# Recurrent layers: v copied to the state partitions by DMA instead of matmuls, the product kept in PSUM, GpSimd's product tied to the next item

## The reference

```
xa = LN(x); sx = shifted xa - xa
xm_j = xa + sx * (maa_stack_j + tanh((xa + sx*maa_x) @ maa_w1)_j @ maa_w2_j)   # j: k, w, v, r, g
w = exp(-exp(time_decay + tanh(xw @ td_w1) @ td_w2)); r, k, v = xr@Wr.T, xk@Wk.T, xv@Wv.T
for t:                                   # a scan over the 100 tokens
    a   = k_t[:, None] * v_t[None, :]    # 16 x 16 per head
    out = r_t . (u * a + s)
    s   = a + w_t[:, None] * s
x1 = x + (head_norm(out) * silu(xg@Wg.T)) @ Wo.T
return x1 + sigmoid(xr2@Wfr.T) * (relu(xk2@Wfk.T)**2 @ Wfv.T)
```

## Time and profile before

| | us |
|---|---|
| median of 3 runs (3709.96 to 3715.34) | 3711.06 |
| the profiled execution | 3714.36 |
| its span in the trace | 3712.5 |
| first layer's recurrence, product of item 1 to product of item 128 | 861.12 to 1620.29 |
| a turn in the middle of a layer | 98.7 to 102.3 |

### The profile page before, as it was taken

How to read it: one execution, slowest core, us unless ns; L and a number is a source line. 1 busy time by engine, 2 the same in 40 slices (tenths; PEclk the granted TensorE clock), 3 DMA queues, 4 the chain that set the end, 5 groups by cost and what they waited for, 6 DMA issues and landing times.

```text
span 3712.5 us, 57293 instructions
## 1 busy us (share of the span) xinstructions
PE 3342.7 (90%) x19200; PEld 2542.2 (68%) x19200; DVE 2232.2 (60%) x5509; ACT 1484.0 (40%) x4241; POOL 791.5 (21%) x532
## 2 busy tenths in 40 slices
PE   7999999978888889968999999999987788998886
PEld 6655656666677777758555555699986577777775
DVE  2888888736788888852355444501001788887873
ACT  1777777651333333225344444412221233333322
POOL 1111112003433343410110100000000443343341
PEclk9999999987899999989999999999998899998998
DMA  2000000110000000010000000200001000000000
GB/s 97 29 20 22 20 28 12 58 53 1 1 1 0 0 0 0 0 47 23 17 25 16 16 24 16 102 24 0 0 1 74 1 1 5 4 4 4 4 5 9
DMA packets 18173, 70.92 MB, mean 19 GB/s; under 512 B 1451, under 2 KB 9195, under 8 KB 14671
## 3 DMA queue, kind: packets, MB, share of 16 engines
q1 hardware_dynamic: 17998, 68.91, 5.1%
HBM read 65.63 MB, written 3.28 MB: 19 GB/s over the span
## 4 chain that ended last, share of the span: by engine, by line
PE 67%; DVE 14%; issue 13%; ACT 5%; DVEq 1%; DMA 0%; SPq 0%; ACTq 0%
PE psum L461 16%; PE psum L272 9%; PE psum L1382 7%; PE psum L1444 5%; PE psum L1327 5%; PE psum L1345 4%; PE psum L475 3%; PE psum L440 3%; PE psum L1390 3%; PE psum L233 2%; PE psum L452 2%; DVE arena L1551 2%; PE psum L248 2%; DVE arena L703 2%; PE psum L468 1%
## 5 line engine op out<-in xcount | busy, mean ns | idle before, releaser
L461 PE MATMUL psum<-arena 128*128 128x200 f32 x4096 | 798.0, 352 | 48.3 <-DVE arena L806 21.0
L461 PEld LDWEIGHTS psum<-arena 128*128 128x128 f32 x4096 | 727.8, 200 | 136.7 <-issue 78.6
L1094 POOL TENSOR_TENSOR arena<-arena 128x800 f32<-128x800 f32 x256 | 485.5, 1897 | 889.4 <-DVE arena L709 889.4
L1679 ACT ACTIVATE arena<-arena 100x361 f32<-100x361 f32 x768 | 460.3, 599 | 465.4 <-DVE arena L1540 460.4
L1382 PE MATMUL psum<-arena 128*100 128x361 f32 x1536 | 609.0, 478 | 17.4 <-DVE arena L1540 14.7
L1540 DVE CUSTOM_DVE_ANT_0 arena<-psum,arena 100x361 f32<-100x361 f32 x768 | 406.5, 530 | 310.4 <-issue 305.7
L709 DVE TENSOR_TENSOR_SCAN arena<-arena 128x808 f32<-128x808 f32 x256 | 507.3, 1982 | 32.0 <-ACT arena L913 22.4
L1390 PEld LDWEIGHTS psum<-arena 100*128 100x128 f32 (+1 forms) x2304 | 301.8, 151 | 244.7 <-issue 122.8
L1722 POOL TENSOR_TENSOR arena<-arena 128x400 f32<-128x400 f32 x192 | 168.0, 908 | 1184.3 <-PE psum L1382 972.4
L272 PE MATMUL psum<-arena 128*128 128x200 f32 (+1 forms) x2048 | 353.1, 335 | 22.0 <-DMA arena<-L_w 20.2
L703 DVE TENSOR_TENSOR arena<-arena,psum 128x800 f32<-128x800 f32 x256 | 251.1, 981 | 197.0 <-PE psum L440 108.8
(11 more groups left out here) (107 smaller groups left out, 3940.6 us busy)
## 6 DMA issues: line engine op xcount, KB each, us to landing
arena<-ctxT SPq DMA_DIRECT2D x32, 722.0 KB, 4.2
arena<-L_w SPq DMA_DIRECT2D x8, 1152.0 KB, 16.1
arena<-L_w SPq DMA_DIRECT2D x8, 1024.0 KB, 11.4
arena<-L_fc SPq DMA_DIRECT2D x4, 1024.0 KB, 7.9
arena<-L_pj SPq DMA_DIRECT2D x4, 1024.0 KB, 15.6
arena<-xT SPq DMA_DIRECT2D x4, 800.0 KB, 9.8
outT<-arena SPq DMA_DIRECT2D x8, 400.0 KB, 3.0
arena<-L_w SPq DMA_DIRECT2D x2, 1536.0 KB, 8.6
```

What stands on the lines that cost most here:

```text
L461: mm = pe.matmul(chunk(bank, j), m.W[n][:, k, c * P:(c + 1) * P], src[:, k, :], start=k == 0, stop=k == C - 1)
L1094: pool.tensor_tensor(sv, sv, rb, ALU.mult).then_inc(sem("r_states"), 1)
L1679: act.activation(pr[k % 8][0:L], sm[k % 4][0:L], ACT.Exp, bias=nmx[0:L, k:k + 1], scale=-1.0, accum_out=den[0:L, k:k + 1]).then_inc(exp_re ...
```

## The change

v is evicted once, into rows with one more column in front (E = L+1 = 101), which holds 0; k gets such a column too, which holds 1. For each item SyncE issues two DMAs (L416): each reads 8 partitions of v (one per head) and writes each of them to 16 partitions of `m.spread[n % 2]`, 1616 bytes a row, 128 rows. There are two such buffers, so the DMAs of item n wait for the product of item n-2. ScalarE's `start(n)` then waits for these DMAs and writes the initial states into the first columns, and VectorE multiplies the two SBUF operands into PSUM (L680), 808 elements instead of 800, and scans from PSUM into the ring (L689). The product now waits for `starts` and for the scan before; the wait for `reduce` moves from the product to the scan. GpSimd's product n waits for the product n+1 of VectorE as well. TensorE loses all of `spread`, ScalarE the eviction `v_high`, VectorE `v_low`. In addition, TensorE's order changes in a few places (the first norm's mean ahead of `reduce(6)`, its variance ahead of `reduce(7)`, the bonus sum ahead of the mixing projection, half of g ahead of the second norm's mean, half of k ahead of its variance), VectorE scales the first norm one item earlier, and ScalarE writes xa ahead of the head norm's logarithm.

```diff
+        self.spread = [r.take(2, 4, E) for _ in range(2)]
+        self.kv = core.psum[:, 0:2, :].rearrange("p a b -> p (a b)")[:, 0:2 * 4 * E]
...
+        def spread(i, first):
+
+            for n in range(16):
+                cc, q, _, t0 = item(n)
+                if n % 8 == 0:
+                    wait(sp, "v", i, cc + 1)
+                if n >= 2:
+                    wait(sp, "kv", i, n - 1)
+                elif not first:
+                    wait(sp, "kv", i - 1, n + 15)
+                for h in range(2):
+                    r0 = 32 * (t0 + h) + HC * q
+                    src = rows(m.v[r0:r0 + HC], cc).rearrange("p a e -> p (a e)").unsqueeze(1)
+                    dst = m.spread[n % 2][:, h].rearrange("p a e -> p (a e)")
+                    sp.dma_start(dst, src.broadcast_to([HC, HS, 4 * E])).then_inc(sem(f"v_spread{n % 2}"), 16)
...
-            def spread(n):
...
+                wait(dve, "starts", i, n + 1)
+                if n:
+                    wait(dve, "states", i, n)
...
+                kb = rows(m.k, cc).rearrange("p a e -> p (a e)").unsqueeze(1).broadcast_to([P, 2, 4 * E])
+                dve.tensor_tensor(m.kv.rearrange("p (h x) -> p h x", h=2), kb,
+                                  m.spread[n % 2].rearrange("p h a e -> p h (a e)"), ALU.mult).then_inc(sem("kv"), 1)
+                wait(dve, "kv", i, n + 1)
...
-                wait(dve, "v_spread", i, n + 1)
-                kb = pairs(m.k, cc).unsqueeze(1).broadcast_to([P, 2, 2 * NB, L])
-                vb = psum[:, 0:2, 0:2 * N].rearrange("p h (a t) -> p h a t", t=L)
-                dst = m.ring[n % 4].rearrange("p (h c) (b e) -> p h (c b) e", h=2, b=NB)[:, :, :, 1:E]
-                dve.tensor_tensor(dst, kb, vb, ALU.mult).then_inc(sem("kv"), 1)
...
-                flat = m.ring[n % 4].rearrange("p j e -> p (j e)")
-                dve.tensor_tensor_scan(flat, m.we[:, cc].rearrange("p j e -> p (j e)"), flat, 0.0,
+                dve.tensor_tensor_scan(m.ring[n % 4].rearrange("p j e -> p (j e)"),
+                                       m.we[:, cc].rearrange("p j e -> p (j e)"), m.kv, 0.0,
                                        ALU.mult, ALU.add).then_inc(sem("states"), 1)
...
-                if n >= 4:
-                    wait(act, "r_states_sum", i, (n - 4) // 2 + 1)
...
+                wait(act, f"v_spread{n % 2}", i, 32 * (n // 2 + 1))
...
                     wait(pool, "states", i, n + 1)
+                    if n < 15:
+                        wait(pool, "kv", i, n + 2)
```

More of the change, by code:

```diff
@@ L488, in body @@
                     wait(pe, "v", i, 1)
-                    wait(pe, "v_low", i, 1)
                 m.n1.pe_mean(pe, lambda c: X[:, c, ds(g + 1, N)], f)
-            spread(1)
+            if back:
+                reduce(6, b)
             if tail:
+                project_half("fr", m.xr2, 1, 5, "ffn_r_sum")
                 wait(pe, "ffn_squared", t, 2)
                 project_half("fv", m.kk, 0, 2, "ffn_v_sum")
-            if back:
-                reduce(7, b)
             if front:
@@ L503, in body @@
                 m.n1.pe_var(pe, f)
-            spread(2)
+            if back:
+                reduce(7, b)
             if tail:
@@ L544, in body @@
                 project_half("v", m.xm[2], 1, 2, "v_sum")
-            spread(6)
             if rec:
                 reduce(1, i)
+                wait(pe, "ruk", i, 4)
+                if back:
+                    wait(pe, "head_log_var", b, 1)
+                else:
+                    pe.wait_ge(m.n1.lnv.sem, m.n1.lnv.at(f, 1))
+                heads(core.heads_w, m.rk, "bonus_sum")
             if front:
@@ L559, in body @@
                 mm.then_inc(sem("mix_hidden_sum"), 1)
[L560 to L565, removed]
-                heads(core.heads_w, m.rk, "bonus_sum")
-            spread(7)
             if back:
@@ L572, in body @@
                     wait(pe, "v", i, 2)
-                    wait(pe, "v_low", i, 2)
                 project_half("o", m.og2, 0, 2, "out_sum")
@@ L590, in body @@
                 wait(pe, "x1", b, 1)
+            if rec:
+                if not back:
+                    wait(pe, "mix_hidden", f, 2)
+                project_half("g", m.xm[4], 0, 3, "gate_sum")
+            if back:
                 m.n2.pe_mean(pe, lambda c: X[:, c, ds(g - 1, N)], b)
-            spread(9)
             if front:
@@ L597, in body @@
             if rec:
-                if not back:
-                    wait(pe, "mix_hidden", f, 2)
-                project_half("g", m.xm[4], 0, 3, "gate_sum")
-            spread(10)
-            if rec:
-                reduce(3, i)
+                reduce(3, i)
+            if front:
+                wait(pe, "mixed", f, 1)
+                if rec:
+                    wait(pe, "gate", i, 1)
+                project_half("k", m.xm[0], 0, 3, "k_sum")
             if back:
@@ L652, in body @@
                 mix(4)
-            spread(14)
             if rec:
@@ L660, in body @@
                     wait(pe, "v", f, 1)
-                    wait(pe, "v_low", f, 1)
                 elif rec:
@@ L797, in body @@
             step(6)
-            if rec:
-                if back:
-                    wait(dve, "v_spread", b, 16)
-                v_low(i, 1, 2)
             if back:
@@ L958, in body @@
                     wait(act, "kv", b, 16)
-                act.activation(half(m.k, 1), full(2), ACT.Copy).then_inc(sem("k"), 1)
+                act.activation(rows(m.k, 1)[:, :, 1:E], full(2).rearrange("p (a t) -> p a t", t=L),
+                               ACT.Copy).then_inc(sem("k"), 1)
+            if front:
+                m.n1.wait_scaled(act, f)
+                if rec:
+                    wait(act, "mixed", i, 5)
+                for c in range(C):
+                    act.activation(m.xs[:, c, :, 1:E], seq(m.n1.yc)[:, c], ACT.Identity, bias=vec("ln1_b", c),
+                                   scale=vec("ln1_w", c)).then_inc(sem("xa"), 1)
             if back:
```

106 lines of the change are left out of this document (37 added, 69 removed).

## The result

| | before | after |
|---|---|---|
| median, us (4 runs each) | 3713.20 | 3849.27 |
| range, us | 3709.96 to 3716.45 | 3846.41 to 3854.18 |
| the profiled execution, us | 3714.36 | 3854.18 |
| its span, us | 3712.5 | 3852.4 |

The change makes the kernel slower: 3849.27 us, a ratio of 1.0368 [1.035, 1.0386]. I had forecast slower, but 4131 us: +417.8 on the 3713.2 of before where +136.1 came.

What follows compares the result with a forecast made beforehand. TensorE (90% busy) bounds the kernel before; afterwards the copy at 7.60 us an item would. 3714.4 + 411.7 for two layers + 8 for their starts = 4134, less 3.3 to the median: 4131 us, range 3620 to 4360.

Steps and rivals of the forecast that it cites:

- What bounds the kernel, and what the change removes: Whole kernel: TensorE tightest at 90%, an item every 5.98 us; `spread` removed, 9.0 us of work a turn, 6.3 on the chain.
- The transfer, mechanism: DMAs of each item: eight concentrated source partitions set the rate, so transfers miss the 5.98 us beat and products wait.
- The transfer, size: DMAs of each item: 54.4 GB/s, 7.60 us an item, adding 206.0 and 205.7 us for the two layers; chance 0.52.
- The start of a layer: First transfer of each layer, which nothing precedes: 4 us a layer, 8 us in all.
- Product and scan: VectorE: product 0.99 us, scan 1.84 from PSUM; GpSimd's held-back product falls on the scan, giving back at most 36 us.
- The turn: A turn with recurrence in the profile after: some 122 us, TensorE busy about 65%.
- The rival on the clock: TensorE's granted clock, 0.93 before, falls as it idles; adds time only below a mean of 0.7; no chance given.
- the transfer is hidden: Rival: copy keeps the 5.98 us beat, 3633 us (3570 to 3670); chance 0.34 together with the latency rival's fast side.
- The starts of ScalarE: Within the hidden-transfer rival: product now behind ScalarE's start, 30 waits at L913 with 0.98 us each, +29 us.
- PSUM with GpSimd's wait: Within the hidden-transfer rival: of the 36 us GpSimd's work costs VectorE's scans, about 10 come back.
- a latency, not a rate: Rival: transfers keep the beat but land late, 3650 to 3720 us; fast side in 0.34, slow side in 0.09, both shared.
- One group at a time: Rival: an item's two DMAs do not overlap, 15.2 us an item, 6053 us; chance of slower than forecast 0.05.

## Why the prediction was right in its mechanism and wrong in its size

**What bounds the kernel, and what the change removes**: right. The item is the beat, and what TensorE and VectorE lose in busy time (99.0 and 119.0 us) does not show in the time while the copy sets the beat.

**The transfer, mechanism**: right. Products wait for L877 and L877 for DMAs; 8 neighbouring source partitions set the rate; the same bytes from rows 4 apart, behind the same waits, take 302 us less, and half the bytes 287 less.

**The transfer, size**: this is the step that failed, in the words of the prediction: "Between them I take two groups of eight in flight, one for each DMA (they read different partitions), 54.4 GB/s and 7.60 us an item." The item took 6.52 us, 63.5 GB/s. The two layers then cost 139 us instead of 411.7, and that is nearly the whole error, 272.6 of the 282 us. Two things in that step were wrong. The two DMAs of an item are not two groups that add up: when the second begins, the rate stays at 45 to 58 GB/s, 50 in the median. And the step looked at one item by itself. The next item reads rows of the other half, and for the length of the handover the rate is 78 to 136 GB/s. The kernel that keeps to one half has 56 GB/s and 4080.5 us, 50 below the forecast; so the alternation of t0 between items, which stands in the code, is worth 231 us. That this kernel comes so near the 7.60 us is in part luck: it too has such handovers, at every second item, and between them its rate is 8% below the 54.4 that I took.

The rule of the Trainium skill was the right one, and I read it only halfway. "SBUF — State Buffer", Door 1: The DMA port swizzle, puts partitions 64 apart on different ports and 32 apart on the same one. The runs agree: 8 neighbours (two ports by that map) stand at 45 to 58 GB/s, 8 rows 16 apart (four ports) at 78 to 158, 8 rows 4 apart (eight ports) at 129 to 200, and the items in turn on both halves pass the 54.4 GB/s that the figure of the Trainium skill gives for two ports. The pieces of up to 158 with rows 16 apart are not the rate of four ports, since the two DMAs of an item read different ones. By the same page of the Trainium skill, "Can I just issue two DMAs to hit both halves?", two such DMAs serialize, and the pair was 6% above a single one. The run agrees in that it is far from twice the rate: 68 GB/s with both halves in each item, after 56 with one half.

**The start of a layer**, 8 us for both: the first product starts at 865.9 instead of 861.1, 4.8 us, and the second layer adds nothing to that. Mis-sized by 3 us.

**Product and scan**: 1.007 us for the 0.99 taken, 1.836 for 1.84. GpSimd's product lies on the scan and neither is slowed. Right.

**The turn**, forecast 122 us with TensorE at 65%, is 104.4 in the mean (16 x 6.52), and 102.5 with TensorE at 81% in the turn shown, by the same error. The granted clock is 0.92 in that turn, 0.93 before. The rival on the clock was right that it falls, and TensorE pays some 72 us of busy time for it; but TensorE is idle in 19% of that turn, and no run shows a part of it in the time.

**The rival "the transfer is hidden"** was wrong for this change, but rows 4 apart make it true, so its price can be read: 3633 forecast, 3547 measured. The removed `spread` was priced by its 6.3 us of one turn's chain, 97 us in all (and its work at 9.0 us a turn, from one piece of the chain, where TensorE is busy with L440 for 10.5 of that turn). With the order of before TensorE loses 170.9 us of busy time (3342.7 to 3171.8) and the span 179.7, while TensorE's share stays at 90%:

```profile
PE 3171.8 (90%) x18176; PEld 2459.3 (70%) x18176; DVE 2113.8 (60%) x5480; ACT 1470.7 (42%) x4209; POOL 762.5 (22%) x532
```

That the two agree is not a price of `spread`: the kernel with the same matmuls gone, but product and scan in SBUF and no wait of GpSimd, gains 10 us. The starts of ScalarE were priced at 29 us; early starts of two items alone bring 46. And PSUM with GpSimd's wait was priced at 10 of 36 us, from the lock as it was before. But the copy to SBUF gives the product a second SBUF operand, and without PSUM and the wait VectorE pays for it: product and scan take 915.0 us in place of the 758.4 of before, and the kernel is at 3703, with them at 3535. Of the 178 us between before and 3535, the exchanged copy by itself brings 10 and these two on top of it 168, on the order of before. The split goes by that sequence: what PSUM and the wait would bring in the kernel before, with `spread` still there, wasn't tried. The Trainium skill has such a contention in "SBUF — State Buffer", Who interferes with whom: a VectorE instruction with two SBUF inputs contends with a GpSimd instruction that reads SBUF. The 1.96 us product agrees, and so does the 1.836 us scan beside GpSimd with one input in PSUM.

**The rival "a latency, not a rate"**: half the bytes, 3563 us, rule it out. **"One group at a time"**, 15.2 us an item, is out by the 6.52.

What stays open: why two DMAs from different halves, issued one behind the other, run side by side only in part. In both kernels at most eight packets are in flight in more than 98% of the time, so two DMAs together have no more packets in flight than one; that this is the reason is not shown.

## What to carry to other kernels

Before a copy inside SBUF replaces matmuls, count which partitions one DMA reads and which the next ones read, not only its bytes: here the same 413.7 KB took 3 us or 6.5 by the distance between 8 source rows. When an operand moves from PSUM to SBUF, look again at every VectorE operation that then reads two SBUF operands beside GpSimd; one operand in PSUM and GpSimd held back onto that operation was worth 168 us here. And price work taken from one engine together with what it puts on the next: the same matmuls gone from a TensorE at 90% brought 10 us while VectorE's product and scan grew by 157, and 178 once they no longer did.

## What the runs showed of the hardware

- A DMA from 8 neighbouring partitions, each read 16 times, stands at 45 to 58 GB/s; rows 16 apart at 78 to 158; rows 4 apart at 129 to 200. In all of them the DMA share is mostly 0.4 to 0.6 while it runs, so hardly more than half of the 16 engines work at a time: 0.432 x 16 = 6.9 engines in after, whose queue is never empty. A packet of 1616 bytes takes 216, 113 and 73 ns in the median.
- Where the next DMA's source rows lie 32 partitions from those of the last one, the rate stays at 50 GB/s at the handover. Where they are other rows, in the same half or in the other, it rises: to 78 to 136 GB/s in after, to 100 with one half.
- Half the bytes a packet (808 instead of 1616) run mostly at 42 to 50 GB/s from the same 8 neighbours, as the full ones do; a packet takes 106 ns in the median.
- An issue on SyncE takes 0.647 us while the queue is short, and 1.28 in the median and up to 4.07 us in after: a full queue is paid in issue time.
- A VectorE product of two SBUF operands that starts 0.65 us into a GpSimd product ends 0.86 us after it (1.96 in all instead of 1.00). GpSimd's, beside a scan of two SBUF operands, takes 3.32 us in the median instead of 1.74.
